# Scores of two neighbouring chunks in one slot and none in the next, in the attention of a float32 transformer block

## The reference

```python
q = split_heads(x @ wq.T) * qk_scale
k = split_heads(x @ wk.T) * qk_scale
v = split_heads(x @ wv.T)
q, k = (_rope(q), _rope(k))
energy = jnp.einsum('bhtd,bhld->bhtl', q, k) + mask
attn = jax.nn.softmax(energy, axis=-1)
out = jnp.einsum('bhtl,bhld->bhtd', attn, v)
return out.transpose(0, 2, 1, 3).reshape(B, T, D) @ wo.T
```

## Time and profile before

| | |
|---|---|
| median of 3 runs | 2360.45 us (2357.5 to 2361.66) |
| profiled execution | 2361.54 us, of it 2359.6 us span from the first to the last instruction |
| TensorE busy, matmuls | 1971.2 us (84%), 14340 instructions |
| VectorE / ScalarE / GpSimd busy | 1491.6 / 1331.8 / 823.7 us |
| scores (L439) | 1280 matmuls, mean 403 ns |
| transposes (L456) | 2176, mean 275 ns |
| products (L474) | 4352, mean 271 ns |
| exponentials (L611) | 640, mean 627 ns, and as many read-outs of 204 ns |

### The profile page before, as it was taken

One profiled execution on the slowest core, in us unless ns is written; L12 is line 12 of the kernel. 1 busy time (PEld: TensorE's weight loads), 2 busy tenths in 40 slices (PEclk: granted clock), 3 DMA queues, 4 the chain that ended last, 5 costly groups with the idle time before them and its releaser, 6 DMA issues. The chain is left out here.

```text
span 2359.6 us, 43734 instructions
## 1 busy us (share of the span) xinstructions
PE 1971.2 (84%) x14340; PEld 1794.1 (76%) x14340; DVE 1491.6 (63%) x3318; ACT 1331.8 (56%) x3381; POOL 823.7 (35%) x937
## 2 busy tenths in 40 slices
PE   5799999999999999999999987501176999999990
PEld 5699988888988888988888876500155999999990
DVE  6655566656566656666666775288864666666655
ACT  4666665666665666665666653200065666666655
POOL 1122333333333333333111110000095666766652
PEclk9999999999999999999999998555598999999995
DMA  1000011001001001000000110300002444454428
GB/s 60 27 10 21 21 30 32 24 28 33 21 30 32 24 28 32 22 30 28 23 26 24 32 32 21 147 0 0 0 0 83 149 143 134 149 167 150 149 52 285
DMA packets 91405, 135.81 MB, mean 58 GB/s; under 512 B 16932, under 2 KB 79376, under 8 KB 87148
## 3 DMA queue, kind: packets, MB, share of 16 engines
q1 hardware_dynamic: 75372, 123.52, 15.2%
q0 software_dynamic: 15872, 10.24, 2.6%
HBM read 104.62 MB, written 39.85 MB: 61 GB/s over the span
## 5 line engine op out<-in xcount | busy, mean ns | idle before, releaser
L474 PE MATMUL out_ps<-v_sb,probs_t 128*128 128x64 f32 x4352 | 551.0, 271 | 17.6 <-DVE attn L773 15.1
L474 PEld LDWEIGHTS out_ps<-v_sb,probs_t 128*128 128x128 f32 x4352 | 532.4, 194 | 27.4 <-DVE probs_t L750 20.6
L736 DVE TENSOR_REDUCE part_max<-scores_ps 128x1 f32<-128x512 f32 (+3 forms) x576 | 356.9, 621 | 205.0 <-PE scores_ps L439 148.8
L611 ACT ACTIVATE probs<-scores_ps,neg_max 128x512 f32<-128x512 f32 (+3 forms) x640 | 398.1, 627 | 45.0 <-DVE neg_max L740 42.7
L439 PE MATMUL scores_ps<-k_st,q_parts 128*128 128x512 f32 (+3 forms) x1280 | 410.8, 403 | 11.4 <-ACT probs L611 5.0
L456 PE MATMUL probs_t_ps<-ident,probs 128*128 128x128 f32 x2176 | 347.6, 275 | 1.0 <-DVE probs_t L750 1.0
L620 ACT COPY probs_t<-probs_t_ps 128x512 f32<-128x512 f32 (+3 forms) x416 | 208.5, 501 | 244.6 <-PE probs_t_ps L456 243.2
L456 PEld LDWEIGHTS probs_t_ps<-ident,probs 128*128 128x128 f32 x2176 | 261.4, 142 | 51.4 <-issue 2.6
L1463 PE MATMUL up_ps<-xe_t,w 128*128 128x320 f32 x1920 | 288.9, 310 | 2.4 <-DVE xe_t L1570 1.7
L1463 PEld LDWEIGHTS up_ps<-xe_t,w 128*128 128x128 f32 x1920 | 283.6, 189 | 3.0 <-issue 1.9
L439 PEld LDWEIGHTS scores_ps<-k_st,q_parts 128*128 128x128 f32 x1280 | 200.5, 193 | 25.2 <-ACT probs L611 7.2
(11 more groups left out here) (214 smaller groups left out, 3153.8 us busy)
## 6 DMA issues: line engine op xcount, KB each, us to landing
w_raw<-in_w_expert SPq DMA_DIRECT2D x32, 1536.0 KB, 6.4
w_raw<-in_w_adapter SPq DMA_DIRECT2D x32, 384.0 KB, 6.9
x_t<-in_x_t SPq DMA_DIRECT2D x64, 128.0 KB, 2.1
x_row<-in_x SPq DMA_DIRECT2D x64, 128.0 KB, 2.0
x_rows<-x SPq DMA_DIRECT2D x64, 128.0 KB, 1.7
acc_rows<-x SPq DMA_DIRECT2D x64, 128.0 KB, 1.8
ln_x<-acc_rows SPq DMA_DIRECT2D x16, 512.0 KB, 6.2
out_rows_dram<-ln_y SPq DMA_DIRECT2D x16, 512.0 KB, 5.2
```

The source lines that it names most:

```text
L474: mm = pe.matmul(o_ps[:, h, :], probs_t[:, g % PT_RING, a - lo:a - lo + P], v_sb[:, slot(b, a // P), h, :], start=a == 0, stop=a == t * P)
L611: act.activation(probs[:, g % PROBS_RING, 0:hi - lo], s_ps[:, g % AHEAD, 0:hi - lo], ACT.Exp, bias=neg_max[:, u % 8:u % 8 + 1], accum_out= ...
L736: red = dve.tensor_reduce(neg_max[:, ring:ring + 1] if single else part_max[:, ring, c:c + 1], s_ps[:, g % AHEAD, 0:hi - lo], AX.X, ALU.ma ...
```

## The change

TensorE's scores are handed out to slots by a new list. `score_slots` gives chunk g the slot `g // 2 * 2 - AHEAD`: an even chunk keeps its slot g-4, and an odd chunk moves from slot g-4 to g-5. An even slot s so issues `scores(s + 4)` and `scores(s + 5)` ahead of `turn(s)`, and an odd slot issues none. A chunk is not taken earlier than the slot after the one in which ScalarE and VectorE read its latest keys (`kt_read`); for this `attention_slots` also notes the slots of the steps that read. Three odd chunks (149, 309, 469) stay where they were by that rule. The orders of the other engines, the buffers and the semaphores are as before.

```diff
--- before.py
+++ after.py
@@ -88,6 +88,15 @@
             if b == NB - 1 and 4 <= n < 8:
                 order.append((b, 7 - n))
     return order
+
+
+def score_slots(total, ready):
+
+    slots, last = [[] for _ in range(total + 3)], 0
+    for g in range(AHEAD, total):
+        last = max(last, g // 2 * 2 - AHEAD, ready[g] + 1)
+        slots[last].append(g)
+    return slots
 
 
 def attention_slots(NB, NT):
@@ -138,6 +147,7 @@
                         continue
                 elif not 0 <= of < count:
                     continue
+                made[k, of] = at
                 if k.endswith("_read") and made[k[:-5], of] < at:
                     early[at].append((k, of))
                 else:
@@ -192,6 +202,10 @@
         u, c = chunks[g]
         b, t = order[units[u][0]]
         return max(nth_projected[b, x] for x in range(4 * c, min(4 * c + 4, t + 1)))
+
+    kt_slot = {k: g for g in range(len(late)) for kind, k in early[g] + late[g] if kind == "kt_read"}
+    scores_at = score_slots(CHUNKS, [kt_slot.get(latest_key(g), -1) for g in range(CHUNKS)])
+    assert sum(scores_at[g].index(x) >= 0 for g in range(len(late)) for x in scores_at[g]) == CHUNKS - AHEAD
 
     def walk(main, step):
 
@@ -476,8 +490,8 @@
                 mm.then_inc(values_done, 1)
 
             def main(g):
-                if g + AHEAD < CHUNKS:
-                    scores(g + AHEAD)
+                for j in scores_at[g]:
+                    scores(j)
                 if g < CHUNKS:
                     turn(g)
                 for j in products_at[g] if g < CHUNKS + 2 else ():
```

## The result

The changed kernel took 2478.44 us (median of 4 runs, 2473.94 to 2480.46), the kernel before 2361.05 us (4 runs too). The ratio is 1.0495, with a 95% interval of 1.0474 to 1.0517: slower by 117 us, where 102 were forecast. The profiled execution took 2473.94 us.

The account below looks back on a forecast made before the run. TensorE was taken to set the end of attention, every wait adding to it. A 40.5 + B 31.6 + C 6.9 + D 2 + E 27 - 5 = 103 us gave 2463 us on the median's scale; range 2400 to 2500.

Parts of the forecast that it names:

- A: Three-chunk units starting at an odd chunk: the moved scores wait for an exponential; 32 places, sum 40.5 us.
- B: First slot of four-chunk units: moved scores wait for an exponential behind a projection step; 44 of 63 late, 31.6 us.
- the clock: Rival 3's claim: new gaps in TensorE's work make its granted clock fall, up to 1.7 us each; not in the sum.
- The deduction of 5 us for earlier maxima: Taken off the sum because some of B is ScalarE's own wait for maxima that would now be earlier.
- C: Three-chunk units with even start: exponentials behind an even slot's transposes, now 0.55 us later; 6.9 us at some 20 places.
- D: Entering and leaving scores: fewer float32 to float32r changes give -8 us, scores that waited +10 at 96 places.
- E: Odd slots without scores lose 0.3 to 0.6 us of cover, so products and projections wait; together +27 us.
- Rival 1: Nothing waits and only entries count, 2352 us, chance 0.04; or TensorE's headroom absorbs all, 2360 us, chance 0.03.
- Rival 2: Only A is real, as ScalarE gains lead in four-chunk tiles: 32 to 40 us, about 2398 us; chance 0.12.
- Rival 3: TensorE's clock falls with the new gaps, up to 1.7 us each; at 30 falls +51, 2515 us; chance 0.14.

Follow-up runs that it names:

- the run with the wait alone: Kernel before, scores in their old slots, plus only a TensorE wait for exp(s+1) ahead of turn(s) in even slots: 2438.47 us, +78.2 us.
- the filled kernel: Changed kernel plus TensorE transposes nobody reads where it would wait (nine at three-chunk places, five at four-chunk places with a step between): 2461.87 us.

## Why the prediction was right

The direction, the mechanism and the range held; the time was 15 us above the forecast value. The two long stalls, A and B, were read to a few per cent. The smaller terms were less good, and they and the clock err in opposite directions.

- **A.** 1.07 us was worked out for slot 232 and 1.05 measured. From the first to the second scores the mean over all 32 places is 1.87 us, so 1.32 lost and 42 us in all, against 40.5. That no stall is won back was shown by the run with A alone.
- **B.** The same distance has a mean of 1.03 us over 64 slots, 0.48 lost, 31 us against 31.6 (the prediction counts 63 slots and 44 late ones; slot 0 is one more). At slots without a step between the exponentials (such as 212) there is no wait, as forecast. The deduction of 5 us for earlier maxima was wrong: none came.
- **C.** 6.9 us were forecast. I find 0.12 us at each of 9 of the 32 slots and nothing at the others, 1 us in all; at slot 248 it is 0.12 where 0.21 was worked out. Perhaps the reserve was counted too small, since ScalarE's queue is emptier there after a stall; no run shows it.
- **D.** After a stall the next group starts 0.57 us behind the scores, as in the earlier trace rows; 78 places and not 96 were late, so this is +8. The saving by fewer entries is seen in the third slots: 3.0 us over 64 places in the run with these alone, 3.9 at the same places in the changed kernel, 0.05 to 0.06 each, near the value taken. (The time of that run, -3.7 with an interval down to -0.5, wouldn't fix it.) In the trace before, the first of the two matmuls of full scores is followed by the second after 0.23 us behind a float32r projection and after 0.32 us behind transposes or products. The Trainium skill (TensorE: Matmul & The Clock Gate, Back-to-back issue gap) gives an isolated matmul of 512 columns a gap of about 216 ns (131 in a stream) and has no term for what stands before it; the first of these distances is near the 216, the second isn't.
- **E.** +27 forecast for the odd slots without scores; 18 to 20 measured, of which the clock has some 5, so this term was about twice too large. The products' waits were seen at 8 of the 18.6 us given to them. In the changed kernel the wait for `attn` rose by 2.0 us, where the prediction named 10 as a sign; the statistics' row rose by 0.8 (6.6 forecast) and that of `q_t` by 3.6 (8 forecast).
- **The clock** was left out of the sum and stood among the rivals. It is the term that was mis-sized: 0 taken, 16.6 us won back by the filled kernel, and some 24 by the runs' means. The earlier trace rows had shown a fall and its price, and the text had named stalls beside other waits as what would bring more. Without these 24 us the loss is 93, and the sum said 103. So it was partly luck that the value came within 15 us: on balance the other terms were 10 us too large (C and E too large, B too small by its deduction), and that hid a part of the missing clock.

Rival 1 (no wait, or headroom in the weight loads) is out by the run with the wait alone: its 72 us of stalls cost 78. Rival 2 (only A) is out: B alone costs 39 us. Rival 3 is half true: the profiled execution has 12 stretches at 1.2 GHz in attention where that of before has 7, and misses 38 us of full clock against 17. That is 21 us, under half of the 51 that I gave it.

## What to carry to other kernels

Ask of an instruction that is moved ahead not only what it needs but what stands behind it in its queue: here the scores could have waited, and the transposes and products behind them could not. To find how early something can be had, follow the written order of the engine that makes it back to the last thing that depends on the waiting engine; the distance between the two in the trace before is the stall. In this case it was right to 0.02 us in slot 232, to some tenths in most others (in one it was 1.2 us short), and the sum over the 96 slots of A and B was 72 us where 73 came. In a chain over three engines, reordering one more of them may only move the wait: here ScalarE's order gave back 51 us of the 117, and VectorE's on top of it 6.

## What the runs showed of the hardware

- Some 70 more short waits of TensorE, most of 0.5 to 1.3 us, brought more time at 1.2 GHz, though the longest single wait for an exponential is 2.9 us: some 24 us of 2478, of which 16.6 were regained by matmuls whose results nobody reads. By the runs with one kind of place each, the 32 stalls of 1.3 us brought some 19 us of it, and the 64 of kind B, 0.5 us on average, hardly 2.
- A float32r matmul that had to wait for a semaphore starts 0.05 us behind the end of ScalarE's read-out, at nearly all of the 77 places of the changed kernel. From such scores to the next group it is 0.57 us, alike in both kernels, in place of 0.46 behind float32r or 0.55 behind float32 groups. In the trace the weight load of such scores starts together with the matmul (both at 1236.57 for those of the earlier trace rows), and 0.23 us ahead of it for those of the earlier trace rows. That this is the reason for the 0.11 us fits, but wasn't tested.
- One change fewer between float32 and float32r groups was worth 0.05 to 0.06 us, where a stall of kind A is 1.3.
